# Weight splits of a batch two tiles ahead of their use, loads reordered, first blocks issued in pairs, one router-bias product

## What is computed

```python
out = jnp.einsum('bsd,bdh->bsh', x, selected_W) + selected_b[:, None, :]
...
probs = jax.nn.softmax(xf.astype(jnp.float32) @ Wr, axis=-1)
eidx = jnp.argmax(probs, axis=-1)
...
h = jnp.maximum(jnp.einsum('ecd,edf->ecf', xe, W1), 0.0)
ye = jnp.einsum('ecf,efd->ecd', h, W2)
...
x = x + _L0_ffn_ref(_L0_cond_ref(x, itok_B_0_63, L0_cond_W, L0_cond_b), L0_ffn_Wr, L0_ffn_W1, L0_ffn_W2)
```

## Time and profile before

| | us |
|---|---|
| median of three runs | 852.15 |
| lowest, highest | 849.8, 856.18 |
| the profiled execution | 854.16 |
| its span, first to last instruction | 852.4 |
| PE busy | 830.8 (97% of the span) |
| DVE busy | 403.3 |
| ACT busy | 251.4 |
| share of PE on the chain that ended last | 96% |

### The profile page before, as it was taken

One profiled execution on the slowest core, in us unless ns is written; L12 is line 12 of the kernel. 1 busy time (PEld: TensorE's weight loads), 2 busy tenths in 40 slices (PEclk: granted clock), 3 DMA queues, 4 the chain that ended last, 5 costly groups with the idle time before them and its releaser, 6 DMA issues.

```text
span 852.4 us, 10964 instructions
## 1 busy us (share of the span) xinstructions
PE 830.8 (97%) x4209; PEld 677.8 (80%) x4209; DVE 403.3 (47%) x552; ACT 251.4 (29%) x345; POOL 229.7 (27%) x238
## 2 busy tenths in 40 slices
PE   8997988999999999999999999999999999999997
PEld 5776775888888888888888888888888888888886
DVE  4465771644354535543455345533653365327431
ACT  3221220433143323332233223322432143215320
POOL 1000001724530363036302730173017302021201
PEclk9998998999999999999999999999999999999999
DMA  9785253473435332633263425342533253225201
GB/s 315 262 300 211 101 190 119 131 252 126 134 117 216 121 127 102 243 117 129 91 246 114 132 91 218 143 136 78 200 150 129 93 191 141 86 107 170 93 0 49
DMA packets 60795, 127.27 MB, mean 149 GB/s; under 512 B 8235, under 2 KB 8235, under 8 KB 60258
## 3 DMA queue, kind: packets, MB, share of 16 engines
q1 hardware_dynamic: 46706, 93.35, 30.4%
q0 software_dynamic: 13488, 32.54, 11.9%
q10 hardware_dynamic: 576, 1.05, 0.4%
HBM read 110.13 MB, written 25.17 MB: 159 GB/s over the span
## 4 chain that ended last, share of the span: by engine, by line
PE 96%; DMA 2%; issue 2%; POOL 0%; DVE 0%; ACT 0%; SPq 0%; POOLq 0%
PE acc_ps L935 41%; PE y_ps L918 41%; PE acc_ps L850 7%; PE tp_ps L850 3%; PE tp_ps L777 1%; DMA stage<-cond_w 1%; PE acc_ps L834 1%; DMA rows<-h_rows,tok_all 1%; PE tp_ps L755 0%; PE y_ps L810 0%; PE y_ps L834 0%; PE tp_ps L834 0%; DMA h_rows<-rows 0%; POOL rows L367 0%; PE acc_ps L838 0%
## 5 line engine op out<-in xcount | busy, mean ns | idle before, releaser
L935 PE MATMUL acc_ps<-xt_split,w_split 128*128 128x512 f32 x1536 | 354.0, 390 | 0.8 <-DVE xt_split L689 0.8
L918 PE MATMUL y_ps<-w_split,xt_split 128*128 128x512 f32 x1536 | 352.1, 389 | 0.0
L935 PEld LDWEIGHTS acc_ps<-xt_split,w_split 128*128 128x128 f32 x1536 | 289.5, 189 | 61.5 <-DVE xt_split L689 1.2
L918 PEld LDWEIGHTS y_ps<-w_split,xt_split 128*128 128x128 f32 x1536 | 288.3, 188 | 59.9
L511 ACT ACTIVATE xt_split<-acc_ps 128x512 fp32r<-128x512 f32 x128 | 76.5, 598 | 417.9 <-PE acc_ps L935 417.9
L713 DVE SCALAR_TENSOR_TENSOR xt_split<-acc_ps,xt_split 128x512 fp32r<-128x512 f32 x128 | 88.6, 692 | 208.2 <-ACT xt_split L511 208.2
L374 POOL DMA_INDIRECT rows<-h_rows,idx_all x112 | 117.2, 1047 | 255.4 <-DVE tp_ps L703 216.9
L624 DVE TENSOR_TENSOR w_split<-stage,w_split 128x1024 fp32r<-128x1024 f32 x66 | 80.9, 1226 | 16.4 <-ACT w_split L459 16.4
L736 DVE SCALAR_TENSOR_TENSOR rows<-y_ps,p_cur,rows 128x512 f32<-128x512 f32 x32 | 24.0, 751 | 133.0 <-PE y_ps L918 133.0
L630 DVE TENSOR_TENSOR w_split<-stage,w_split 128x1024 fp32r<-128x1024 f32 x64 | 78.5, 1227 | 16.4 <-ACT w_split L465 16.4
L406 POOL DMA_INDIRECT out<-rows,put_all x32 | 31.4, 982 | 154.3 <-DVE rows L736 154.3
(11 more groups left out here) (111 smaller groups left out, 247.0 us busy)
## 6 DMA issues: line engine op xcount, KB each, us to landing
stage<-w SPq DMA_DIRECT2D x64, 1024.0 KB, 6.6
b_rows<-x SPq DMA_DIRECT2D x8, 1024.0 KB, 7.7
h_rows<-rows POOLq DMA_DIRECT2D x7, 1024.0 KB, 6.6
stage<-cond_wt SPq DMA_DIRECT2D x4, 1024.0 KB, 5.9
x_more<-x_t SPq DMA_DIRECT2D x4, 1024.0 KB, 8.7
stage<-x_t SPq DMA_DIRECT2D x3, 1024.0 KB, 6.6
stage<-cond_w SPq DMA_DIRECT2D x3, 1024.0 KB, 8.3
rows<-h_rows,idx_all POOLq DMA_INDIRECT x112
```

What stands on the lines that cost most here:

```text
L918: last = nc.tensor.matmul(y_ps[:, s, :], hts[:, j % HB, a, s * P:(s + 1) * P], w2s[:, q % 2, w, jj, :], start=(j == 0 and (a, w) == (HI, HI)),
L935: last = nc.tensor.matmul(acc_ps[:, j % 2, :], w1s[slot][:, w, k, jj * P:(jj + 1) * P], xts[:, par, a, k, :], start=(k == 0 and (w, a) == ...
```

## The change

The tables `SPLIT_X` and `SPLIT_W` are rewritten: the four W splits of batches 1, 2 and 3 stood at tiles (5, 5, 6, 7), (13, 13, 14, 15) and (21, 21, 22, 23), and stand now at (4, 4, 5, 5), (10, 11, 12, 12) and (16, 17, 17, 20). The x splits of chunks 2 to 7 stood at (4, 5), (8, 9), (12, 13), (16, 17), (20, 21), (24, 25) and stand at (3, 4), (6, 7), (10, 11), (15, 16), (20, 21), (22, 24). SP's loads are written out in a new order. Of the four first blocks of x, ACT's queue issues two and SP's queue the other two, between the blocks of W(0). The bias products of all four batches are made once, in `m_turn(0)`, ahead of the weight products and with four columns instead of one.

```diff
-    SPLIT_X = [None, None] + [(TPC * (c - 1), TPC * (c - 1) + 1) for c in range(2, NCH)]
-    SPLIT_W = [None] + [tuple(2 * TPC * b - n for n in (3, 3, 2, 1)) for b in range(1, BATCH)]
+    SPLIT_X = [None, None, (3, 4), (6, 7), (10, 11), (15, 16), (20, 21), (22, 24)]
+    SPLIT_W = [None, (4, 4, 5, 5), (10, 11, 12, 12), (16, 17, 17, 20)]
...
-        bias_g = sb("bias_g", [P, 2], f32)
+        bias_g = sb("bias_g", [P, BATCH], f32)
...
-        bias_ps = y_ps[:, 3, P:P + 1]
+        bias_ps = y_ps[:, 3, P:P + BATCH]
...
             for k in range(DK):
+                if k >= DK // 2:
+                    sp.dma_start(stage[:, 2, k, :], xt_v[:, k, 0:CH]).then_inc(s_x0[k], 16)
                 sp.dma_start(stage[:, 1, k, :], cond_view(0)[:, k, :]).then_inc(s_w0[k], 16)
...
-            for b in range(2, BATCH):
-                load_next_xt(CPB * b)
-                load_next_xt(CPB * b + 1)
-                sp.wait_ge(s_turn, b)
-                load_cond_wt(b)
+            def load_cond(b):
                 sp.wait_ge(s_wlo, DK * b)
                 sp.dma_start(stage[:, 1, :, :], cond_view(b)).then_inc(s_stage[1], 16)
                 load_bias_rows(b)
 
+            load_next_xt(4)
+            load_cond(2)
+            load_next_xt(5)
+            sp.wait_ge(s_turn, 2)
+            load_cond_wt(2)
+            load_next_xt(6)
+            load_next_xt(7)
+            load_cond(3)
+            sp.wait_ge(s_turn, 3)
+            load_cond_wt(3)
...
-                                     bias=bias_g[:, (c // CPB) % 2:(c // CPB) % 2 + 1]).then_inc(s_ltc, 1)
+                                     bias=bias_g[:, c // CPB:c // CPB + 1]).then_inc(s_ltc, 1)
...
-            for k in range(DK):
+            for k in range(DK // 2):
                 act.dma_start(stage[:, 2, k, :], xt_v[:, k, 0:CH]).then_inc(s_x0[k], 16)
...
-                nc.vector.tensor_copy(m32[:, b % 2, :, :].rearrange("p k g -> p (k g)"), m_ps)
-                nc.vector.tensor_copy(bias_g[:, b % 2:b % 2 + 1], bias_ps).then_inc(s_mcopy, 1)
+                if b == 0:
+                    nc.vector.tensor_copy(bias_g[:, :], bias_ps)
+                nc.vector.tensor_copy(m32[:, b % 2, :, :].rearrange("p k g -> p (k g)"), m_ps).then_inc(s_mcopy, 1)
...
+                if b == 0:
+                    for k in range(DK):
+                        for g in range(NQ):
+                            nc.tensor.matmul(bias_ps[g * G:(g + 1) * G, :], wr32[:, k, :], b_col[:, :, k],
+                                             start=(k == 0), stop=(k == DK - 1))
                 for k in range(DK):
                     for g in range(NQ):
-                        nc.tensor.matmul(turn_ps[g * G:(g + 1) * G, :], wr32[:, k, :],
-                                         stage[:, 0, k, g * P:(g + 1) * P], start=(k == 0), stop=(k == DK - 1))
-                for k in range(DK):
-                    for g in range(NQ):
-                        last = nc.tensor.matmul(bias_ps[g * G:(g + 1) * G, :], wr32[:, k, :], b_col[:, b, k:k + 1],
-                                                start=(k == 0), stop=(k == DK - 1))
+                        last = nc.tensor.matmul(turn_ps[g * G:(g + 1) * G, :], wr32[:, k, :],
+                                                stage[:, 0, k, g * P:(g + 1) * P], start=(k == 0), stop=(k == DK - 1))
```

## The result

The changed kernel takes 831.99 us (median of 4 runs, 831.89 to 832.36) against 851.49 us before (849.8 to 856.18): a ratio of 0.9772, 95% interval 0.9745 to 0.9799, 19.5 us less. The forecast was 834.5 within 831.5 to 842.

What follows compares the result with a forecast made beforehand. PE, on the chain for 96% of the span, was taken as the bound. Gaps 13.6, bias product 0.8 and start 3.4 sum to 17.8 us less; from the 852.15 median that gives 834.3, stated as 834.5, range 831.5 to 842.

Steps and rivals of the forecast that it cites:

- The three gaps: PE's waits ahead of tiles 8, 16 and 24 for late W splits; removing them with their slow tiles gains 13.6 us.
- The slow tiles: Tiles 16 and 24 take 5.46 and 4.45 us instead of 2.77, at a low clock; they vanish with the gaps.
- Slack 7 us: Load of W(3) lands by 67, ACT wants it at 74.2, so it is 7 us early.
- 1.5 us and more: Slacks claimed for the new order of splits, as the argument against a new wait replacing one gap.
- rival 2: A new wait of PE in the first stage takes the place of one gap, 7.2 us: 841.5; chance 0.13.
- the walk: Going through the new order of splits and loads with the old durations to find what could be late next.
- Cost 0: SP's new load order holds later loads behind its waits, but they are wanted late enough: no time lost.
- The bias product: Bias products leave m_turn(1), (2) and (3), 0.28 us each on the chain: 0.8 us gained.
- The start: First blocks issued in pairs: W(0)'s first block lands 1.7 us earlier and 1.7 us of slow clock go: 3.4 us.
- the upper bound: At the start, W(0)'s first block lands at 6.0, first matmul right behind the zeros at 7.12: 3.7 us gained.
- the clock term of 1.7: Slow clock behind PE's idle time at the start, from 9.13 to 22.01, cost 1.7 us and would go.
- Rival 1: Changed issue at the start gives nothing, since all queues share the 16 DMA engines: 837.7; chance 0.22.

Runs made afterwards that it cites:

- b2: Changed kernel with the third and fourth W split of batch 2 put back to tiles 14 and 15; 846.39 us (kernel before beside it 857.82).
- b1: Kernel before, plus matmuls on zeros filling PE's waits ahead of tiles 16 and 24, splits left late; 851.97 us (kernel before beside it 857.82).
- c1: Kernel before, unchanged, run and profiled a second time; 851.92 us.
- a4: Changed kernel with SP's loads in the order of before; 832.41 us (kernel before beside it 850.77).
- a2: Changed kernel with all four first blocks of x issued by ACT's queue at once again; 834.02 us (kernel before beside it 850.77).
- c4: The kernel of a2 with 28 instead of 20 matmuls on zeros at the gather; 833.7 us (kernel before beside it 852.37).
- c2: Changed kernel, unchanged, run and profiled a second time; 832.16 us (kernel before beside it 852.37).
- a1: Kernel before with only the changed kernel's two split tables and SP load order; 836.23 us (kernel before beside it 850.77).
- b3: Changed kernel with the third and fourth first block of x issued by ACT's queue behind its first split; 838.43 us (kernel before beside it 857.82).
- a3: Changed kernel with the bias product made batch by batch again; 835.68 us (kernel before beside it 850.77).
- b4: Changed kernel with 12 instead of 14 matmuls on zeros at the start; 838.15 us (kernel before beside it 857.82).

## Why the prediction was right, and where not

**The three gaps.** Right in place and cause. The size, 13.6, was met against the profile that it was made from (13.8 with the splits alone); against the second profile of the same kernel it is 11.3, and what differs is the slow tiles. b2 shows the cause at tile 16 by putting it back. I did not undo the splits at tiles 8 and 24 one by one; for those the cause is read from the rows, and that they went.

**The slow tiles.** b1 shows that they were the clock. But I treated 4.4 us of slow tiles and 1.7 us of slow start as part of each execution. They are not: of these 6.1 us the second profile has 1.6, all at tile 16. That the first profile had them all is luck, and the forecast had no term for it. The sum was made against an execution whose span was 5.0 us above that of c1. The average share can be read from the runs' own clocks. The kernel before ran 7 times beside the a kernels: its quickest run, 846.22 us, had a mean granted clock of 0.998, its slowest, 854.02, had 0.986. The changed kernel's runs are all at 0.998 or 0.999. So, as an estimate from the quickest run (846.22 less 832), of the 19.5 us some 14 are waits and work removed, and the other 5 to 6 an average over falls of the clock behind PE's idle time.

**What was next late.** "Slack 7 us" for W(3): the load was issued at 54.33 and took 9.4 us at most, so it was there by 63.7; ACT wanted it at 67.90. Slack 4.2, cost 0 as said. The W splits of batch 1 were done at 28.1, 5.0 us before tile 8 (forecast: about 6), those of batches 2 and 3 about 8 us before tiles 16 and 24. The slack of "1.5 us and more" that rival 2 is held against stands nowhere in the walk. "Cost 0" for the load order is a4's 0.

**The bias product.** 0.8 forecast, 0.91 measured.

**The start.** The step that was mis-sized. Forecast 3.4: 1.7 for an earlier block (6.65) and 1.7 for the clock. Measured by undoing it: 1.94 in the traces of a2 and after, 1.06 between c4 and c2. The block came earlier than forecast (by 5.96, where the upper bound had 6.0), so the zeros, ending at 7.22, became the bound; but the clock term of 1.7 was luck of the first profile: none of the five other profiles of kernels that issue as before at the start (a1, a2, b1, c1, c4) shows a fall there. Rival 1 (the start gives nothing, 837.7) did not come. The rule cited for it, from the Trainium skill ("DMA: Bandwidth & Descriptors", "Issuing engines are not separate DMA queues"), agrees with b3: the queue did not matter. What I drew from it, a gain of at most 0.5 us, does not follow, since the moment of issue changed as well and decides what stands ahead.

**What the sum lacked.** The gather (2.05 us) and the start of the second stage (1.7 us at a clock of 0.50 up to about 153 us before). The forecast said that the second stage keeps its length. It was 703.05 and 703.2 in the two profiles of the kernel before and 701.3 to 701.4 in all other profiles of the first, the a and the c runs. Against the medians, the start was over-sized by 1.5 to 2.3 us and the falls of the clock at the gather and elsewhere were missing; the two errors went in opposite directions, which is why 834.5 is only 2.5 off, and that they nearly cancel is luck; 0.7 of the 2.5 is the median of before, 851.49 and not 852.15. The measured time lies near the low end of the range, because that end held only the spread of single runs and nothing for the gather. Its own terms, 834.5 less 0.3 and less 2.35, give 831.85 and not 831.5; the measured 831.99 is above either by little.

## What to carry to other kernels

A split, copy or conversion that the next phase waits for belongs ahead, in the engine's order, of everything that waits for products of the phase now running; look at what is queued in front of the last one, not at when its data came. A short idle of TensorE has a fixed price, its length, and a varying one, the clock behind it: several profiles of one kernel, or the granted clock of each timed run, tell them apart, and a kernel without such waits is not only faster but steadier. When two transfers are under way at once, ask which must land first and issue the other later, on whatever queue: here two blocks issued 2 to 2.7 us later let the block that PE needed first land 1.4 to 2.6 us earlier.

## What the runs showed of the hardware

The same wait need not have the same price. PE idle for 2.88 us before tile 24: clock 0.50 behind it in one execution, 1.00 in another. Idle for 2.2 us at the gather: 1.00 in both profiles of the changed kernel; for 2.1 us in a2: 0.59 over 4 us. Idle for 2.01 us at the start: 0.50; for 1.89: 1.00. Idle for 1.84 us before tile 8: 1.00 in all three profiles that have it. Idle for 4.5 us before tile 16: it fell to 0.50 both times, for all of the tile once and for about two thirds of its 4.34 us the other time. Runs of the kernel before spread over 8 us, those of the changed kernel over 1.2. The rise at the start varies too: the same 14 matmuls on zeros, begun at 1.55 us, took 4.68 us in a3, 5.66 in the first profile of the changed kernel and 6.15 in a1, so they ended at 6.2 to 7.7. The Trainium skill ("TensorE: Matmul & The Clock Gate", "What's actually happening") says that the moment of the ramp differs from run to run of one kernel; these runs agree.

Left open: why the gather took 15.2 to 15.3 us in both profiles of the kernel before and in a1, and 13.2 to 14.0 in the rest. In the kernel before, the late landing of one gathered block (5.1 us) is part of it; in a1 the gathered blocks took 3.5 to 3.7 us, and the late one is the store ahead of them, the last rows of the first stage, with 3.8 us where it took 2.0 in the kernel before and the changed one. The low clock is another part; between a2 and c4 the gather differs by 0.4 us. What delays a transfer in some executions I did not try. Nor is it shown why the clock fell at the gather in a1, a2, a3 and b4, whose tiles had no waits, and not in after, c2, a4, b3 and b2. The stage ended at 115.3 to 115.8 us in four of those without a fall and at 116.3 to 118.3 in those with one, but at 121.5 in b2, which has none, and nothing here varied that moment alone. The fall is part of a3's 3.3 us in the median; how large a part was not measured.
